# A decoder layer's last attention: score blocks in twos, their weighted sums in twos one group behind

## What is computed

```
q, k   = heads of x @ w_q, x @ w_k            # 8 heads of 64
gates  = sigmoid(x @ w_gate); gm = gates at the best of 8 experts, else 0
values = einsum('bhne,ehdk,bnd->bhnk', gm, value_experts, x)
attn   = softmax(where(causal, (q * 64**-0.5) @ k.T, lowest))
out    = attn @ values
out    = einsum('bhne,ehkd,bhnk->bhnd', gm, output_experts, out).sum(heads)
```

## Time and profile before

| what | us |
|---|---|
| median of 3 runs (lowest to highest) | 936.79 (936.63 to 937.72) |
| the profiled execution, its own time | 937.28 |
| its span, first to last instruction | 934.3 |
| PE busy | 897.4 (96%) |
| DVE busy | 628.6 (67%) |
| POOL busy | 316.2 (34%) |
| ACT busy | 307.8 (33%) |

### The profile page before, as it was taken

How to read it: one execution, slowest core, us unless ns; L and a number is a source line. 1 busy time by engine, 2 the same in 40 slices (tenths; PEclk the granted TensorE clock), 3 DMA queues, 4 the chain that set the end, 5 groups by cost and what they waited for, 6 DMA issues and landing times.

```text
span 934.3 us, 15873 instructions
## 1 busy us (share of the span) xinstructions
PE 897.4 (96%) x6316; PEld 668.3 (72%) x6316; DVE 628.6 (67%) x940; ACT 307.8 (33%) x494; POOL 316.2 (34%) x309
## 2 busy tenths in 40 slices
PE   6989999999999999999999998999999999999998
PEld 3668778877745444889976785888776445449998
DVE  4767566467554657978868574765774555778887
ACT  3645555210154445201133355641002443450000
POOL 5212412222375778356610023210005544771000
PEclk9999999999999999999999999999999999999999
DMA  8104000433143643366530000012222010216562
GB/s 272 38 22 136 1 1 1 142 99 112 60 136 88 210 135 76 104 176 187 159 118 1 2 1 1 2 53 90 67 81 79 1 26 2 68 37 179 177 198 91
DMA packets 46719, 80.07 MB, mean 86 GB/s; under 512 B 13047, under 2 KB 24023, under 8 KB 46647
## 3 DMA queue, kind: packets, MB, share of 16 engines
q1 hardware_dynamic: 46647, 79.07, 27.9%
HBM read 59.55 MB, written 19.33 MB: 84 GB/s over the span
## 4 chain that ended last, share of the span: by engine, by line
PE 83%; DVE 8%; issue 3%; ACT 2%; DMA 2%; POOL 1%; SPq 0%; POOLq 0%; DVEq 0%; ACTq 0%
PE ps L1213 19%; PE ps L1587 10%; PE ps L1492 6%; PE ps L1520 5%; PE ps L1432 5%; PE ps L1593 5%; PE ps L1386 5%; PE ps L1221 5%; PE ps L1338 3%; PE ps L1456 3%; PE ps L1400 3%; PE ps L1353 3%; DVE region L1057 2%; PE ps L1255 2%; PE ps L1292 2%
## 5 line engine op out<-in xcount | busy, mean ns | idle before, releaser
L611 POOL TENSOR_TENSOR xT<-xT,region 128x1024 f32<-128x1024 f32 (+5 forms) x80 | 127.7, 1596 | 92.2 <-PE ps L1520 63.8
L1132 DVE COPY_PREDICATED region<-region,ps 128x512 f32<-128x512 uint32 x112 | 82.5, 736 | 66.5 <-PE ps L1213 65.9
L1587 PE MATMUL ps<-expert_hi,k_hi 128*128 128x256 f32 x512 | 126.1, 284 | 0.7 <-DVE k_hi L1116 0.6
L1587 PE MATMUL ps<-expert_lo,k_hi 128*128 128x256 f32 x512 | 124.7, 281 | 0.0
L1057 DVE TENSOR_REDUCE region<-ps 128x2 f32<-128x1024 f32 (+2 forms) x96 | 89.0, 956 | 46.6 <-PE ps L1466 27.7
L1213 PE MATMUL ps<-expert_hi,wide_hi 128*128 128x512 f32 x256 | 102.3, 400 | 0.0
L1213 PE MATMUL ps<-expert_hi,wide_lo 128*128 128x512 f32 x256 | 99.9, 390 | 0.0
L1213 PE MATMUL ps<-expert_lo,wide_hi 128*128 128x512 f32 x256 | 99.8, 390 | 0.0
L1587 PEld LDWEIGHTS ps<-expert_hi,k_hi 128*128 128x128 f32 x512 | 97.3, 190 | 3.4 <-issue 3.4
L1587 PEld LDWEIGHTS ps<-expert_lo,k_hi 128*128 128x128 f32 x512 | 97.4, 190 | 0.0
L1116 DVE TENSOR_TENSOR k_hi<-region 128x1024 fp32r<-128x1024 f32 x64 | 80.7, 1262 | 19.9 <-PE ps L1593 19.7
(11 more groups left out here) (157 smaller groups left out, 1718.9 us busy)
## 6 DMA issues: line engine op xcount, KB each, us to landing
region<-hot_rows SPq DMA_DIRECT2D x128, 128.0 KB, 3.3
expert_hi<-halves_kept SPq DMA_DIRECT2D x22, 384.0 KB, 3.5
expert_lo<-halves_kept SPq DMA_DIRECT2D x22, 384.0 KB, 4.2
halves_kept<-expert_hi SPq DMA_DIRECT2D x16, 512.0 KB, 5.4
halves_kept<-expert_lo SPq DMA_DIRECT2D x16, 512.0 KB, 6.2
expert<-in_value_experts SPq DMA_DIRECT2D x8, 512.0 KB, 4.5
expert<-in_output_experts SPq DMA_DIRECT2D x8, 512.0 KB, 4.5
gb<-scale_rows SPq DMA_DIRECT2D x16, 256.0 KB, 3.9
```

Source lines behind the costliest of these rows:

```text
L611: pool.tensor_tensor(acc(c)[:, heads, lo:CH], acc(c)[:, heads, lo:CH], PT[:, k % RING, heads, lo:CH], ALU.add).then_inc(sem["added"], 1)
L1132: dve.copy_predicated(V3[:, t].rearrange("p (h k) -> p h k", k=HD3), chosen.unsqueeze(2).broadcast_to([P, H3, HD3]), ps[:, n % 4, :].rearr ...
L1587: mm(ps[:, 4 + t // 2, t % 2 * D:(t % 2 + 1) * D], k_hi[n % 2][:, t * P:(t + 1) * P], w[:, slot, columns], start=(n == 0 and t % 2 == 0 an ...
```

## The change

On PE the blocks of a pair are now taken in twos: T(1) T(2), W(0) W(1), T(3) T(4), W(2) W(3) and so on up to T(9) T(10), W(8) W(9); then X, T(11), and for the next pair T(0). W(10) and W(11) stand behind the first two P of the next pair. All four P stand between T(0) and T(1). Of the nine rounds S, the odd ones stand ahead of a T of two and the even ones between the T and the W, and their contents are in another order. `sums(p, 0)` comes ahead of W(4). X additionally waits for the last round, since the joining of the maxima (line 1062) is now behind round 6 of 0 to 8.

On the other queues: pieces at blocks 2, 6, 10; roundings at (2,4), (2,5), (3,2), (3,4); DVE's first masks of the output experts at blocks 2 and 3 of the last pair in place of 5 and 6; normalising of pair 0 and 1 at block 0 of pair 2 and 3, and of pair 2 behind the last addition; ACT copies the last pair's results before it rounds pair 2; `max_row` moves past nothing, it is written one block later. On PE `sums(3, 1)` stands behind all high products of the first output step.

The diff, cut to its core:

```diff
-        ROUNDS = [[(0, 0), (2, 0)], [(1, 0), (5, 1)], [(3, 0)], [(4, 0)], [(5, 0)], [(6, 0)],
-                  [(4, 1), (6, 1)], [(7, 0)], [(7, 1)]]
+        ROUNDS = [[(1, 0), (5, 1)], [(4, 0)], [(5, 0)], [(6, 0)], [(4, 1), (6, 1)], [(7, 0)], [(7, 1)],
+                  [(0, 0), (2, 0)], [(3, 0)]]
-        PIECES_AT = {(0, 2): 8, (0, 5): 9, (0, 8): 10, (1, 2): 11, (1, 5): 12, (1, 8): 13, (2, 2): 14, (2, 6): 15}
+        PIECES_AT = {(0, 2): 8, (0, 6): 9, (0, 10): 10, (1, 2): 11, (1, 6): 12, (1, 10): 13, (2, 2): 14, (2, 6): 15}
-        ROUND_AT = {(2, 7): 0, (2, 9): 1, (3, 2): 2, (3, 3): 3}
+        ROUND_AT = {(2, 4): 0, (2, 5): 1, (3, 2): 2, (3, 4): 3}
-        MASKED_AT = {5: 0, 6: 1}
+        MASKED_AT = {2: 0, 3: 1}
+        ROUND_AHEAD = {3: 1, 5: 3, 7: 5, 9: 7}
+        ROUND_BEHIND = {2: 0, 4: 2, 6: 4, 8: 6, 10: 8}
+        COMBINED_AT = 6
+        NORMALISED_AT = {(2, 0): 0, (3, 0): 1, (3, 11): 2}
...
+                outputs(PAIRS3 - 1, 1)
                 for k in range(len(ROUND_AT), NC * (PAIRS3 - 1)):
                     rounded(k)
-                outputs(PAIRS3 - 1, 1)
...
-                    if m == NR - 1:
-                        until(dve, "s_max", b, (p + 1) * NR)
+                    if m == COMBINED_AT:
+                        until(dve, "s_max", b, p * NR + m + 1)
...
                     until(pe, "tile_max", b, p + 1)
+                    until(pe, "s_max", b, (p + 1) * NR)
...
-                    for u in range(NB):
+                    transposed(p, 0)
+                    for n in range(NC if more else 0):
+                        project(p + 1, n)
+                    if p:
+                        weigh(p - 1, NB - 2)
+                        weigh(p - 1, NB - 1)
+                    for n in range(NC, 2 * NC if more else 0):
+                        project(p + 1, n)
+                    for u in range(1, NB - 1, 2):
+                        if more and u in ROUND_AHEAD:
+                            scores(p + 1, ROUND_AHEAD[u])
                         transposed(p, u)
...
+                        transposed(p, u + 1)
+                        early = SUMS_AT.get(u + 1) == 1
+                        if early and p:
+                            sums(p - 1, 1)
+                        if more and u + 1 in ROUND_BEHIND:
+                            scores(p + 1, ROUND_BEHIND[u + 1])
+                        if u + 1 in SUMS_AT and not early:
+                            sums(p, 0)
+                        weigh(p, u - 1)
+                        weigh(p, u)
+                    if more:
+                        max_rows(p + 1)
+                    transposed(p, NB - 1)
+                weigh(PAIRS3 - 1, NB - 2)
                 weigh(PAIRS3 - 1, NB - 1)
...
-                            sums(PAIRS3 - 1, 1)
                             until(pe, "o_sb", b, PAIRS3 * NC)
                         for t in range(TT) if n else (2, 3):
                             high(t)
+                        if n == 0:
+                            sums(PAIRS3 - 1, 1)
```

More of the change, by code:

```diff
@@ L831, in _ @@
                         weights(p, u)
-                        if p + 1 < PAIRS3 and u in PROJECT_BEFORE:
-                            projected_high(p + 1, PROJECT_BEFORE[u])
-                        if p and u == 0:
-                            outputs(p - 1, 1)
+                        if u == 0:
+                            for n in range(2 * NC if p + 1 < PAIRS3 else 0):
+                                if p and n == NC:
+                                    outputs(p - 1, 1)
+                                projected_high(p + 1, n)
+                            if p == PAIRS3 - 1:
+                                outputs(p - 1, 1)
                         if u == ENDS[0]:
                             outputs(p, 0)
-                        if p + 1 < PAIRS3 and u in PROJECT_AFTER:
-                            projected_high(p + 1, PROJECT_AFTER[u])
                         if u in SUMS_AT and (p or SUMS_AT[u] == 0):
@@ L1115, in masked_high @@
                         until(dve, "mo_used", b, n - 1)
+                    until(dve, "oT_ready", b, NC * (p + 1))
                     dve.tensor_tensor(k_hi[i][:, :], oT[:, p, :], masks[:, n % MASKS, :], ALU.mult
@@ L1144, in _ @@
                         if p + 1 < PAIRS3:
-                            for at in (PROJECT_BEFORE, PROJECT_AFTER):
-                                if u in at:
-                                    projected_low(p + 1, at[u])
-                            for m in ROUND_OF.get(u, ()):
-                                maximum(p + 1, m)
-                            if u == ROW_AT:
-                                max_row(p + 1)
-                        elif u in RINGED:
-                            add_up(u)
+                            if u == 0:
+                                if p:
+                                    max_row(p)
+                                for n in range(2 * NC):
+                                    projected_low(p + 1, n)
+                            for at in (ROUND_AHEAD, ROUND_BEHIND):
+                                if u in at:
+                                    maximum(p + 1, at[u])
+                        else:
+                            if u == 0:
+                                max_row(p)
+                            if u in RINGED:
+                                add_up(u)
                         if p and u == (4 if p == PAIRS3 - 1 else 5):
@@ L1157, in _ @@
                             (masked_high, masked_low)[MASKED_AT[u]](0)
-                        if p and u == NORMALISED_AT[p]:
-                            normalise(p - 1)
+                        if (p, u) in NORMALISED_AT:
+                            normalise(NORMALISED_AT[p, u])
                 for n in range(NEP):
```

20 lines of the change are left out of this document (1 added, 19 removed).

## The result

The changed kernel takes 923.47 us, the median of four runs (922.63 to 925.0), against 937.08 (936.63 to 937.72) for the kernel before on the same chip. The ratio is 0.9859, 95% interval 0.9844 to 0.9875: 13.6 us faster. The forecast was 925.0, in a range of 914 to 932. The profiled execution took 925.0 us, its span is 922.9; it is the slowest of the four, with a mean granted clock of 0.993 where the other three (922.63 to 924.24 us) have 0.996.

A forecast was written before the change was run, and what follows sets the result against it. PE, busy 96% of the span, was taken as the bound. Per item 9.6 us saved, less 3.6 or 2.2 of waits and 0.5 behind the stage: 12.4 off the profiled 937.3 gives 924.9, said as 925, range 914 to 932.

The forecast's parts named there:

- round 3, three times: PE's wait between rounds 2 and 3: 0.8 us in each of three pairs, and 0.1 between rounds 1 and 2.
- joining: DVE's joining of maxima, moved between the maxima of rounds 6 and 7: 1.2 us in two pairs, 0.3 in the third.
- row maxima, three times: PE's wait for row maxima at the pair's end: 0.3 us per pair, as before.
- sums(2, 1), item 1: PE waits 0.5 us ahead of sums(2, 1) in item 1 for POOL's additions, which start later behind W(4).
- the same chain, item 0: POOL's late additions ahead of sums(2, 1) in item 0, where the experts' piece adds 2.36 us: 2.8 us.
- The saving: PE's changes of tile shape in an item's heads stage fall from 118 to 60: 9.6 us per item less matmul time.
- the rule weighed against it in the prediction: Weight loads overlap matmuls only where row groups differ, so T behind T pays 0.10, 2.3 us less saved; not taken.
- rival 2's first half: T behind T pays 0.10 on PE, 4.6 us in two items; the whole rival had a chance of 0.18.
- POOL's run: POOL's additions from block 5 on take 14.9 us in all; PE reaches sums(2, 1) about 14.5 after W(4).
- rival 3: Slower: POOL paces the heads stage, each of four pairs in both items pays 2.3 us, so 949 us; chance 0.05.
- the signs named: Among signs of being right: joinings of 2 us, PE waiting ahead of rounds 3 and 8, stages of 119 to 123 us.
- The tail: Behind the heads stage, waits on a chain from the last denominators: 0.5 us charged per item, bounds -0.3 and 1.5.

The follow-up runs named there:

- e1: The changed kernel with the W of the last pair one at a time again: 921.99 us, ratio 0.985 to the kernel before.
- e7: The kernel before with the new tables alone (round contents, joining behind round 6, pieces at even blocks), blocks not in twos: 935.58 us, ratio 0.9997.
- e8: The changed kernel with sums(p - 1, 1) between round 2 and the W behind it, scaling of those denominators at block 7: 922.75 us, ratio 0.985.
- e6: The changed kernel with sums(p, 0) behind W(4) and W(5) instead of ahead of them: 923.28 us, ratio 0.9853.
- e5: The changed kernel with the third pair's two roundings one block earlier, at blocks 3 and 4: 920.75 us, ratio 0.9827.
- e4: The changed kernel with DVE's first two output-expert masks at blocks 5 and 6 of the last pair, as before: 926.59 us, ratio 0.9909.
- f7: e5 with sums(3, 0) behind W(4) and W(5) in the last pair alone: 919.67 us, ratio 0.9826.
- e2: The changed kernel with the maxima joined behind the last round again: 924.85 us, ratio 0.9876.

## Why the prediction was right, point by point

| term, us | predicted | measured in the changed kernel |
|---|---|---|
| matmul time of a stage | 122.0 to 112.3 | 112.3 in item 1, by starts |
| start of pair 0 | 0.3 | 0.21 |
| round 3, three times | 0.8 and 0.1 | 0.59 and 0 |
| joining | 1.2, 1.2, 0.3 | 0.1 each |
| row maxima, three times | 0.3 | 0.34 (item 0 twice, its third lies in the 1.49) |
| sums(2, 1), item 1 | 0.5 | 1.47 |
| the same chain, item 0 | 2.8 | 4.2 (1.49, 0.44, 2.26) |
| sums(3, 0), both items | none | 1.25 |
| clock | none | 1.64 in item 0's stage |
| small steps, most at rounds | none | 0.9 and 0.9 |
| stage above 112.3, items 0 and 1 | 9.4 and 7.1 | 11.0 and 6.9 |
| output experts, per item | +0.5 | -1.2 and +1.8; +0.5 and +0.1 without the half clock |

**The saving** was right. e1 measured its price apart: ten changes put back cost 1.58 us. T behind T has no bubble, so the row was the better guide than the rule weighed against it in the prediction (by that rule the stages would be 2.3 us longer), and rival 2's first half falls. e7 excludes that the gain came from the tables that it has.

**Round 3** was 0.2 too dear: round 2 to round 3 now takes 1.82 us (295.87 to 297.69), not 1.90, and of that 1.23 are work, not 1.14. The wait is there in every pair, as forecast. e8 showed its cause: 0.9 us of sums between the two rounds leave 0.13.

**The joining** is the term that was mis-sized most, by 2.4 us an item. The mechanism is as described (e6: 1.68 us, ending with POOL's operation, and a wait of 0.41 behind it), but the phase was guessed as the bad one. In the first two pairs of the changed kernel it falls on the seam of two POOL operations or close to one; that is luck. In the third pair it takes 1.44 us, and PE loses 0.17 ahead of round 8, since there is slack. The prediction gave 0 to 2.2 as bounds; the value was near the lower one. POOL's phase follows W(4) and the rounds' times follow PE too, so in the first two pairs both repeat, and either both are lucky or none is: e6 moved POOL by 0.88 us, and all six joinings changed.

**POOL's run** was mis-sized the other way. PE reaches sums(2, 1) 14.4 us behind the start of block 5's addition, as forecast (14.5), but POOL needs 15.8 where I had 14.9: 0.08 us pass between any two of its operations and the narrow additions take 4.5, not 4.1. What the wait costs in item 0 was spread over three places, since a ring slot that waits for an addition stops the exponentials as well. e5 took 1.23 of item 1's 1.47 us away by two roundings in another place, which shows the chain; of item 0's 4.2, where the experts' piece stays in the run, it took 0.93.

**sums(3, 0)** is a wait that the prediction missed. The prediction charged the early masks of the last pair nothing in the stage, and wrote in rival 3 that no row prices additions beside DVE's work there. It was in fact this: 3.67 us for two operations of POOL that take 1.75 alone (e4). The Trainium skill's SBUF — State Buffer, "SBUF: two separate sides", describes a lock that an operation of DVE with two SBUF inputs and one of POOL that reads SBUF hold against each other for a whole instruction. The trace agrees: the masks, the rounding and the addition have such inputs, and POOL's two end 1.15 and 0.31 us behind the masks. It decided 1.25 us an item, not the time of the kernel. Rival 3 needed waits for POOL in all pairs.

**The sum** came out right (925.0 for the profiled execution, 924.9 forecast) in part because errors offset each other: joinings -2.4 and rounds -0.9 an item, POOL's waits +1.4 and +1.0, sums(3, 0) +1.25, the small steps +0.9, and the clock +1.6 in item 0. That it came out to 0.1 us is luck: the profiled execution has four stretches at half clock where that of before, from which the sum starts, has two, up to 3.4 us. The three executions with the clock of before took 922.63 to 924.24 us, so against these the forecast was 1 to 2 us too high. What decided the case, 19.2 us of matmul time against waits that could be bounded, didn't hang on these. Two of the signs named did not come: the joinings took 0.17 to 1.44 us and not 2, and PE did not wait ahead of round 8 by more than 0.17.

**The tail** I had as a chain that gives back 0.5 an item; together it gave back 0.6, not 1.0. The split over the items is the clock's: each kernel's profiled execution has one stretch at half clock in these parts, up to 1.7 us, before in item 0 and after in item 1, and without it the items gave back 0.5 and 0.1. The longest pieces of the chain of waits of the changed kernel in item 1, from the masks of the first output steps to the seventh step (start, duration, what):

```profile
828.09 2.23 DVE k_hi L1119
830.32 1.15 DVE q_hi L1126
...
832.62 2.51 DMA scale_rows<-region
...
835.67 4.13 DMA gb<-scale_rows
...
841.33 2.30 POOL wide_lo L600
...
845.01 1.24 DVE q_hi L1126
846.29 1.21 PE ps L1609 x8
```

The wait of 1.55 to 1.57 us at its end stands in every kernel here, before and after the earlier trace rows. A shorter stage moves the chain's start as well as its end, so an earlier PE does not wait longer there, though the prediction said that it would. What grew is the wait one step earlier for masked high halves: 0.69 and 0.78 us, where item 0 had none and item 1 0.14 before.

## What to carry to other kernels

Matmuls of different tile shapes cost at the change, 0.05 to 0.12 us each here; count the changes in the order of the program, price them from start to start in the trace, and group pieces of one shape as far as the buffers allow. Where grouping delays what another engine waits for (here POOL's run of additions), look for work in that engine's queue that can go into the idle time ahead of it: two entries of one table gave 3 us more by the medians, 2.3 of them as waits in the stages. A short operation that shares its data's memory with a long one costs by its phase, not by its length, so bound it and don't bet on it.

## What the runs showed of the hardware that I had not expected

- A 128x8 operation of DVE took from 0.17 to 2.23 us, in kernels with the same instructions. Where I set it beside POOL's queue, it ended with POOL's running operation, or at once where that was ending.
- The lock acts the other way too: an addition of 128 columns on POOL took 1.52 us beside a mask of DVE, 0.46 without.
- Half clock for 3.41 us followed PE's waits in some executions and not in others. In the changed kernel a wait of 2.26 us ahead of sums(2, 1) had it. In f7 a wait of 2.24 at the same place and one of 1.57 in the tail had none, as the windows at their ends show:

```profile
351.60:355.00 3.40, 3.40 (x28) 1.62 (x30) 1.24 (x2) 1.26 (x3) 1.28 (x1) 1.00 0.44 118
838.40:841.80 3.40, 3.38 (x26) 3.21 (x27) 3.40 (x4) 0.00 (x0) 0.00 (x0) 1.00 0.52 163
```

What tells them apart stays open: ahead of the changed kernel's there had been waits of 1.49 and 0.44 us a few us earlier, 0.56 and 0.44 in f7. These don't decide it either: e2 had 1.57 us at X and 2.2 at sums(2, 1) without the stretch, e6 had 0.75 at T(3, 0) and 2.2 at sums(2, 1) with it.
